# Byte addresses of the feed-forward operands, and TensorE's feed-forward tiles as a loop or written out

## The reference

```python
x = layernorm(x + attention(x))      # delta rule in chunks of 32, three FIRs, softmax gates, rmsnorm, @ Wo.T
h = silu(lin(x, w1) ) * lin(x, w2)   # 256 -> 1024, lin(x, w) = (x @ w.T) * column scale
h = gelu(lin(h, h1))                 # 1024 -> 1024
h = gelu(lin(h, h2))                 # 1024 -> 1024
x = layernorm(x + lin(h, w3))        # 1024 -> 256
```

## Time and profile before

| what | us |
| --- | --- |
| runs | 2358.66, 2364.56, 2373.68 (median 2364.56) |
| profiled execution | 2356.63 |
| its span, first to last instruction | 2354.8 |
| TensorE matmuls busy | 2119.6 (90%) |
| VectorE busy | 1156.1 (49%) |
| ScalarE busy | 865.5 (37%) |
| GpSimd busy | 533.9 (23%) |

### The profile page before, as it was taken

How to read it: one execution, slowest core, us unless ns; L and a number is a source line. 1 busy time by engine, 2 the same in 40 slices (tenths; PEclk the granted TensorE clock), 3 DMA queues, 4 the chain that set the end, 5 groups by cost and what they waited for, 6 DMA issues and landing times.

```text
span 2354.8 us, 41749 instructions
## 1 busy us (share of the span) xinstructions
PE 2119.6 (90%) x16936; PEld 1766.1 (75%) x16936; DVE 1156.1 (49%) x1819; ACT 865.5 (37%) x1406; POOL 533.9 (23%) x563
## 2 busy tenths in 40 slices
PE   7888873775999888699999999999999999999998
PEld 5676763665887777488888788788788788788786
DVE  5777768963588676424234323324323332332432
ACT  4445541010343333244334434434433443343442
POOL 1112787864565555200000000000000000000000
PEclk9999996797899899799999999999999999999999
DMA  5766667876999998100000000000000000000000
GB/s 160 201 187 184 190 196 174 264 234 230 223 248 217 221 219 193 63 1 13 6 19 18 1 18 18 1 18 19 1 18 18 19 1 18 19 1 19 18 1 18
DMA packets 247025, 217.32 MB, mean 92 GB/s; under 512 B 159042, under 2 KB 210754, under 8 KB 242242
## 3 DMA queue, kind: packets, MB, share of 16 engines
q1 hardware_dynamic: 234562, 184.30, 28.8%
q10 hardware_dynamic: 12288, 30.41, 4.5%
HBM read 130.52 MB, written 84.15 MB: 91 GB/s over the span
## 4 chain that ended last, share of the span: by engine, by line
PE 56%; issue 1%; DVE 1%; ACT 0%; DMA 0%; POOL 0%; DVEq 0%; SPq 0%; ACTq 0%; POOLq 0%
PE B L1572 50%; PE O L1599 5%; PE T L1530 1%; DVE yb L1698 0%; ACT gate L1637 0%; DMA x<-x_s 0%; DVE stats L1729 0%; DVE xl L1678 0%; DVE z L1724 0%; DVE z L1720 0%; ACT L1637 0%; DVE z L1743 0%; ACT xh L1625 0%; POOL rstd L1779 0%; DVEq L1693 0%
## 5 line engine op out<-in xcount | busy, mean ns | idle before, releaser
L1572 PE MATMUL B<-act0h,wr 128*128 128x512 f32 x1024 | 404.5, 395 | 0.0
L1572 PE MATMUL B<-act1h,wr 128*128 128x512 f32 x1024 | 404.5, 395 | 0.0
L1572 PE MATMUL B<-act1l,wr 128*128 128x512 f32 x1024 | 404.5, 395 | 0.0
L1572 PE MATMUL B<-act0l,wr 128*128 128x512 f32 x1024 | 404.5, 395 | 0.0
L1651 ACT ACTIVATE yb<-B,scol 128x512 f32<-128x512 f32 x256 | 176.5, 689 | 608.0 <-PE B L1572 608.0
L1686 DVE TENSOR_TENSOR act0l<-yb,act0h 128x512 fp32r<-128x512 f32 x256 | 176.3, 689 | 391.2 <-ACT act0h L1654 389.1
L1776 POOL TENSOR_TENSOR rstd<-mv,ln_eps 128x4 f32<-128x4 f32 x16 | 3.2, 201 | 1349.3 <-DVE mv L1737 1349.3
L453 DVE SCALAR_TENSOR_TENSOR acc<-proj,taps,acc 128x512 f32<-128x512 f32 x288 | 214.4, 750 | 86.7 <-ACT acc L399 78.2
L1686 DVE TENSOR_TENSOR act1l<-yb,act1h 128x512 fp32r<-128x512 f32 x128 | 88.7, 693 | 309.1 <-ACT act1h L1654 309.1
L1572 PEld LDWEIGHTS B<-act1h,wr 128*128 128x128 f32 x1024 | 192.2, 188 | 46.7
L1572 PEld LDWEIGHTS B<-act0l,wr 128*128 128x128 f32 x1024 | 192.2, 188 | 46.7
(11 more groups left out here) (169 smaller groups left out, 3202.0 us busy)
## 6 DMA issues: line engine op xcount, KB each, us to landing
qk_s<-yT SPq DMA_DIRECT2D x16, 1024.0 KB, 6.0
kk_s<-kfull SPq DMA_DIRECT2D x16, 1024.0 KB, 6.5
qk<-qk_s SPq DMA_DIRECT2D x32, 512.0 KB, 6.2
wraw<-in_ffn_w ACTq DMA_DIRECT2D x32, 352.0 KB, 5.6
toe<-in_toe_short ACTq DMA_DIRECT2D x32, 320.0 KB, 7.5
xt<-in_xt SPq DMA_DIRECT2D x16, 524.0 KB, 4.4
k_s<-ktok SPq DMA_DIRECT2D x16, 512.0 KB, 7.3
v_s<-vtok SPq DMA_DIRECT2D x16, 512.0 KB, 3.2
```

Of the source, the lines that this page charges most:

```text
L1572: last = nc.tensor.matmul(B[slot % 4][:, :], w, part, start=(k == 0 and i == 0), stop=(k == kts - 1 and i == len(parts) - 1))
```

## The change

Three edits. A tile `align_wr` of 24 floats (96 bytes), never used, is allocated before `wr`; a tile `align_x` of 40 floats (160 bytes), never used, before `xh`. TensorE's loop over tiles 0 to 13 stays in the general branch; in the branch that runs, a Python loop writes the 14 tiles out one after the other, so that semaphore values are constants. The instructions of a tile and their order stay.

```diff
@@ -1440,6 +1440,7 @@
         fast = Stage(nc, sems)
         with fast.ctx:
             wr = keep["wr"]
+            fast.sb("align_x", [P, 40])
             xh, xl = fast.sb("xh", [P, KT, TOK], f32r), fast.sb("xl", [P, KT, TOK], f32r)
@@ -1601,12 +1602,19 @@
+                def two_tiles(i, general):
+                    for p in range(2):
+                        layers(i * 2 + p, general)
+                        turn(1 - p, i + p)
+                        last_layer(i * 2 + p, general)
+
                 def emit(general):
-                    with pe.Fori(0, STEPS // 2 - 1) as i:
-                        for p in range(2):
-                            layers(i * 2 + p, general)
-                            turn(1 - p, i + p)
-                            last_layer(i * 2 + p, general)
+                    if general:
+                        with pe.Fori(0, STEPS // 2 - 1) as i:
+                            two_tiles(i, True)
+                    else:
+                        for i in range(STEPS // 2 - 1):
+                            two_tiles(i, False)
                     layers(STEPS - 2, general)
@@ -1814,6 +1822,7 @@
             with late.ctx:
 
+                late.sb("align_wr", [P, 24])
                 keep["wr"] = late.sb("wr", [P, W_END], f32r)
```

## The result

The changed kernel took 2328.16 us, the median of 4 runs (2321.72 to 2337.43), beside 2367.67 for the kernel before (4 runs). The ratio is 0.9844, 95% interval 0.9817 to 0.9872: 1.6% faster, some 37 us, where 2353 was forecast with a range from 2336 to 2374. In a second set of runs it was 2324.47 us, ratio 0.9849 (0.9822 to 0.9876).

What follows compares the result with a forecast made beforehand. TensorE alone was taken to bound the feed-forward stage; TensorE, VectorE and DMA the delta stage. The terms -11.0 - 3.8 + 0 + 0 + 3 = -11.8 us took the median 2364.56 to 2353 us; range 2336 to 2374.

Steps and rivals of the forecast that it cites:

- The loop written out: Feed-forward stage: removing six jump gaps saves 11.0 us and the slower tiles behind them 3.8, together 14.8 us.
- The weights, price 0: Matmuls of the feed-forward stage: moving the weights from 160 to 0 modulo 256 bytes changes nothing, 0 us.
- Rival 2: Multiplication: aligned operands bring back about 19 ns a matmul, 97 us plus about 10 from L1599; 2246 us; chance 0.09.
- The delta stage, price 3 us: Delta stage: moving its tiles from 128 to 224 makes rows of `tt` straddle 256-byte blocks, 3 us more.
- rival 1: Delta-stage DMAs: a transfer costs the bytes from the 256-byte boundary below its start; 51 us more, 2401 us; chance 0.11.
- the upper end: Delta stage: each straddling packet costs the fixed 8.2 ns twice, 0.52 us a group, 16.8 us over 32 groups.
- The lower end: Delta stage: `wraw` goes from 32 to 128, 100 packets a group saving 8.2 ns each, 2 us less.
- The sum: Whole kernel: -11.0 - 3.8 + 0 + 0 + 3 = -11.8 us, predicting 2353 us.

Runs made afterwards that it cites:

- loop_only: The kernel before with only TensorE's tiles written out and no pads, all addresses as before: 2347.31 us, ratio 0.9956.
- align_only: The kernel before with both pads added and TensorE's loop kept: 2345.19 us, ratio 0.9954.

## Why the prediction was wrong, step by step

**The loop written out: right.** 14.8 us was forecast from the gaps and the slower tiles behind them. `loop_only` gave 14.8 in the trace; its runs gave 10 us, 6 to 14, which is a little less. The clock stays at 1.00 where the first gap was. The estimate that no more code is fetched was on the safe side: 51 blocks against 67.

**The weights, price 0: wrong, and the step that failed.** It gave 31.3 us (`align_only`), of which 5120 x 6.6 ns = 34 us gained and 1024 x 2.4 ns = 2.5 us lost. The argument was that L1572 and L1599 are a misaligned stationary and a misaligned moving operand, and lose the same per column. It took for granted that an operand counts by itself. The runs show that the distance counts, and there both forms of before were unequal, at 96 and 160: the comparison held no case of distance 0 and could not speak about it. That the loss per column came out alike was a coincidence: at distance 0 a matmul of 512 columns is at its fastest, and one of 256 columns at its slowest (0.1199; 0.1136 at 192). Equal duration of the weight loads, 188 ns, said nothing either; they stay at 188 in L1573 while the spacing falls. This step carries the miss: had the weights been worth 0, the time would have been some 2359 us, inside the range.

**Rival 2: right in kind, wrong in size.** It had the whole difference to half of the slow clock's spacing as its prize, 107 us. And the last layer, from which it expected 10 us, lost 2.5. The fastest spacing found is 226.7 ns. The Trainium skill, TensorE: Matmul & The Clock Gate, section "Wait — 56ns, not 53.3ns?", gives 215.7, 11 less than was measured; no run here shows what holds the rest.

**The delta stage, price 3 us: too low.** Its first load came 14.7 us later in the changed kernel, 10 to 20 in the pairs above. The packets became 3.5 ns longer on average (29.3 to 32.8), and about 328 of them a group on each engine make 1.1 us; times 32 that is 37 us of DMA time, of which less than half reached the span. That TensorE and VectorE share the bound, as rival 1's counter-argument said, fits this but was not tested. I had priced straddling rows of `tt` alone, and taken a fifth of 16.8 us because no byte was added; the upper end was nearer. The lower end, 2 us less for `wraw`, had no ground: its rows of 2,816 bytes touch 12 blocks of 256 bytes from offset 32 and from 128 alike, and they are not in the main queue.

**Rival 1: its price near, its mechanism not.** Its own sum had 4.9 ns a packet and 51 us; measured were 3.5 ns and 14.6 us. That the 3.5 ns equal the estimate from the rule of the Trainium skill, DMA: Bandwidth & Descriptors, section How a descriptor splits into AXI transactions, is luck. By that rule, bytes from the boundary below the start, offsets 32 and 64 would be cheaper than 128, and the traces show 32.0 and 31.5 ns against 29.3. The rule is stated for reads, and nearly all these packets write to SBUF.

**The sum.** -14.8 - 31.3 + 14.6 is -31.5, and the spans differ by 31.0. Forecast was -11.8: two errors of 31 and 12 us, opposite in sign. That the forecast came within 25 us of the result is owed in part to the second hiding a part of the first.

## What to carry to other kernels

Before using two rows of one profile as a test of a cause, ask whether the quantity that would matter takes a different value in both; here both had a distance other than 0. An unused tile put ahead of one tile moves all behind it: look at what a stage with full DMA engines gets from that, and give it a pad of its own. Here a pad that put it back to 128 was worth as much as the loop, and offset 0 more. A gap at a loop's jump is read off the chain of waits, with the slower stretch behind it; here that sum held in the trace.

## What the runs showed of the hardware

- The spacing of float32r matmuls of 512 columns, with 128 columns of weights loaded for each, depends on the distance of moving and stationary start modulo 256 bytes: 226.7 ns at 0, 229 at 64, 232 to 234 at the other multiples of 32, at a granted clock of 1.00. For 256 columns 0 is the worst of those seen: 119.9 ns, against 117.4 to 118.9 at 160 and 113.6 to 118 at 192. That two reads of SBUF get into each other's way is a guess that fits; it wasn't tested.
- SBUF tiles at offset 0, 128 and 224 gave 27.5, 29.3 and 32.8 ns a packet in a stage with mostly small packets, and the stage ended 15 us earlier or later for each step, by the means of four traces each; traces of one offset lie up to 15.5 us apart.
- A jump back in a hardware loop of some 1,600 TensorE matmuls and loads costs 1.7 to 2.0 us, and the tiles behind six jumps took 3.8 us more in all, 2.6 of it behind the first and the last, where the granted clock was 0.76 for 7 us.
